# A split first transfer, a rounding moved to VectorE, and another order of the narrow products

## The chip, the cores and the metric

The kernel runs on one core of a Trainium2 chip. Times are microseconds on the device (us). A run's time is that of one execution of the program; the span of a profile runs from its first to its last instruction.

## What is computed

The input x has 128 samples of 32 heads by 512 values. Two residual steps follow each other. The first adds a linear map with a low-rank correction whose factor A is picked by each sample's label. The second adds, for each head, a causal convolution along the 512 values with a kernel K of that head, a skip term, and a mask by each sample's length.

```python
x = x + (einsum('bsi,oi->bso', x, W)
         + 0.5 * einsum('bsr,or->bso', einsum('bsi,bir->bsr', x, lora_A[label]), lora_B_w))
K = 2.0 * einsum('hn,hnl->hl', Ct, exp(P)).real          # one kernel of 512 taps per head
y = irfft(rfft(x, 1024) * rfft(K, 1024))[..., :512] + x * D[:, None]
x = x + y * (arange(512)[None, :] < length[:, None])[:, None, :]
```

## The kernel before

The 512 values of a head lie in four chunks of 128 on the partitions (CH = 4, P = 128), and the 128 samples are the free axis. So every product is a 128x128 weight tile against a moving tile of 128 columns for each (head, chunk) pair. To keep precision, each fp32 operand is split in two fp32r parts, a rounded one (`_hi`) and the rest (`_lo`), and a product is three: hi by hi, lo by hi, hi by lo.

**The start.** W is not used as it comes. TensorE first multiplies A of label 0 by B for each chunk c (the fold, `fold_ps[c]`, four tiles of 32 rows each, read from the one tile `ab_raw`), and VectorE adds half of it to W's chunk (`w_raw`, the scalar_tensor_tensor in `split_chunk`). Chunk 0 of W is added in two halves of 256 columns (`w_parts`), the others in one piece. ScalarE rounds each piece to `w_hi` and x's chunk to `x_hi` (`split_chunk_hi`), VectorE takes the rests `x_lo` and `w_lo`. TensorE's first stage, `chunk(0)` to `chunk(3)`, multiplies these for the first group of four heads. `chunk(0)` waits for `x_hi` of chunk 0 and the first half of `w_hi`, and before its third product for the second half of `w_hi`. The loads of `ab_raw` and then of x's four first chunks stand on SyncE's queue, those of W on ScalarE's.

**Pass 1** goes on over eight groups of four heads with products of 512 columns. Meanwhile K is made on VectorE, ScalarE and GpSimd and stored to `k_pad` in memory.

**Pass 2** (`pass2`) takes the 32 heads one by one. For each the Toeplitz tiles `t_hi` and `t_lo` stand in four blocks by lag, and `xs_hi`, `xs_lo` are the moving parts. The block of lag 0 meets 512 columns, lag 1 384, lag 2 256 and lag 3 128, all summed in one PSUM bank of the pair `y2_ps` (which the profile calls `k_ps`). Lag by lag, three products each: twelve products and twelve weight loads a head. The last head is written out apart, in two halves. VectorE merges a head's sum into x under the mask, and SyncE stores it.

The order on each engine is as the code is written; engines wait for each other by semaphores alone.

Of the kernel before, what the change touches and what calls it, by code (L numbers as in the profile page):

```python
# [13 lines left out]
P = 128  # L14
H = 32
L = 512
CH = L // P
NLAB = 5
RANK = 32
# [10 lines left out]
GH = 4  # L30
GROUPS = H // GH
HALF = L // 2
RAW, TR, XR, LEAD = 4, 5, 4, 3
# [13 lines left out]
def conditioned_residual(nc, xt, idx, wt, a_lab, ab, log_dt, ssm, d_skip, out):  # L47
    ctx = ExitStack()
    with ctx:
# [6 lines left out]
        def sem(name):  # L56
            return ctx.enter_context(nc.semaphore(name))


        x_all = sb("x_all", [P, H, L])  # L60

        x_hi = sb("x_hi", [P, 2 * GH, L], F32R)
        x_lo = sb("x_lo", [P, 2 * GH, L], F32R)

        xs_hi = sb("xs_hi", [P, XR, L], F32R)
        xs_lo = sb("xs_lo", [P, XR, L], F32R)
# [9 lines left out]
        ab_raw = sb("ab_raw", [P, P + L])  # L76
# [49 lines left out]
        t_hi = sb("t_hi", [P, TR, L], F32R)  # L126
# [13 lines left out]
        x_load = [sem(f"x_load{g}") for g in range(1, GROUPS)]  # L140
        w_load = [sem(f"w_load{c}") for c in range(CH)]
        a_load = sem("a_load")
        ab_load = sem("ab_load")
        idx_load = sem("idx_load")
        prm_load = sem("prm_load")
        t_load = [sem(f"t_load{i}") for i in range(RAW)]
# [14 lines left out]
        w_lo_done = sem("w_lo_done")  # L161
        dve_own = sem("dve_own")
        masks = sem("masks")
        x_hi_done = sem("x_hi_done")
        x_lo_done = sem("x_lo_done")
        x_used = sem("x_used")
# [40 lines left out]
        def cols(c):  # L207
            return slice(c * P, (c + 1) * P)
# [5 lines left out]
            return slice(GH * (g % 2), GH * (g % 2) + GH)  # L214


        def split_count(g):
            return CH + 2 * g


        def w_parts(c):
            return ((1, slice(0, HALF)), (2, slice(HALF, L))) if c == 0 else ((c + 2, slice(0, L)),)
# [11 lines left out]
        @block.sync  # L234
        def _(sp):
            def load_x(g):
                sp.dma_start(x_all[:, heads_of(g), :], xt[:, heads_of(g), :]).then_inc(x_load[g - 1], 16)

            sp.dma_start(ab_raw[:], ab).then_inc(ab_load, 16)
            for c in range(CH):  # L240
                sp.dma_start(x_all[:, 0:GH, cols(c)], xt[:, 0:GH, cols(c)]).then_inc(x0_load[c], 16)
            for half in range(2):
                rows = slice(NST * half, NST * half + NST)
                sp.dma_start(logs[rows, 1, :], ssm[:, 0, :]).then_inc(prm_load, 16)
                sp.dma_start(prm[rows, :, :], ssm[:, 1:4, :]).then_inc(prm_load, 16)
            sp.dma_start(logs[:, 0, :], log_dt.rearrange("(o h) -> o h", o=1).broadcast_to([P, H]))\
                .then_inc(prm_load, 16)
            sp.dma_start(d_all[:], d_skip.rearrange("(o h) -> o h", o=1).broadcast_to([P, H])).then_inc(prm_load, 16)
            load_x(1)
            sp.dma_start(idx_i[:], idx.rearrange("(o t) b -> o t b", o=1).broadcast_to([P, 2, P])).then_inc(idx_load, 16)  # L250
            for g in range(2, GROUPS):
                load_x(g)
            sp.wait_ge(consts, 3)
            sp.dma_start(k_pad[:, L:PADK], zeros[:]).then_inc(zeros_stored, 16)

            sp.wait_ge(k_out, 1)
            for j in range(HG):
                rows = k_pad[j:H:HG, 0:L].rearrange("g (a b) -> a g b", b=LB)
                sp.dma_start(rows, k_sb[LA * j:LA * j + LA, :, LB * j:LB * j + LB]).then_inc(k_stored, 16)
            sp.wait_ge(k_stored, 16 * HG)  # L260
            sp.wait_ge(zeros_stored, 16)

            def load_t(k):

                if k >= RAW:
                    sp.wait_ge(t_lo_done, k - RAW + 1)
                window = bass.AP(k_pad.tensor, k * PADK, [[1, P], [1, L]])
                sp.dma_start(t_raw[:, k % RAW, :], window).then_inc(t_load[k % RAW], 16)


            AHEAD = RAW + TR - 2
            for k in range(AHEAD):
                load_t(k)
            for h in range(LAST):
                if AHEAD + h < H:
                    load_t(AHEAD + h)
                sp.wait_ge(o_done, h + 1)
                sp.dma_start(out[:, h, :], x_all[:, h, :]).then_inc(out_stored, 16)
            sp.wait_ge(o_done, H)
            sp.dma_start(out[:, LAST, HALF:L], x_all[:, LAST, HALF:L]).then_inc(out_stored, 16)  # L280
            sp.wait_ge(o_done, H + 1)
            sp.dma_start(out[:, LAST, 0:HALF], x_all[:, LAST, 0:HALF]).then_inc(out_stored, 16)
            sp.wait_ge(out_stored, 16 * (H + 1))
# [127 lines left out]
        def _(act):  # L411
# [3 lines left out]
                act.dma_start(w_raw[:, c, :], wt[cols(c), :]).then_inc(w_load[c], 16)  # L415

            def split_chunk_hi(c):
                act.wait_ge(x0_load[c], 16)
                s.copy(x_hi[:, 0:GH, cols(c)], x_all[:, 0:GH, cols(c)]).then_inc(x_hi_done, 1)
                for n, o in w_parts(c):  # L420
                    act.wait_ge(w_sum, n)
                    s.copy(w_hi[:, c, o], w_raw[:, c, o]).then_inc(w_hi_done, 1)
# [5 lines left out]
                split_chunk_hi(c)  # L428
            act.wait_ge(a_diffed, 1)
            s.copy(a_hi[:], a_diff[:]).then_inc(a_hi_done, 1)  # L430
            act.wait_ge(ab_load, 16)
            s.mul(b_stack[:], ab_raw[0:3 * RANK, P:P + L], LORA_SCALING).then_inc(b_hi_done, 1)

            def split_x_hi(g, pair):
# [86 lines left out]
        def _(pe):  # L521
# [8 lines left out]
            pe.wait_ge(consts, 2)  # L530
            for c in range(CH):
                mm(fold_ps[c][:, cols(c)], ident[:], ident2[:], start=True, stop=False, skip_group_check=True)
            pe.wait_ge(ab_load, 16)
            for c in range(CH):
                r = slice(RANK * c, RANK * c + RANK)
                mm(fold_ps[c], ab_raw[r, 0:P], ab_raw[r, P:P + L], start=False, stop=True,  # L536
                   skip_group_check=True).then_inc(folded, 1)
# [24 lines left out]


            def chunk(c):
                pe.wait_ge(x_hi_done, c + 1)
                for d in range(CH):
                    if c > 0 or d % 2 == 0:
                        pe.wait_ge(w_hi_done, c + 2 if c > 0 else d // 2 + 1)
                    mm(by_head(y_ps[:, d, :]), w_hi[:, c, cols(d)], moving(x_hi, 0, c), start=(c == 0), stop=False,  # L569
                       skip_group_check=True)  # L570
                pe.wait_ge(x_lo_done, c + 1)
                for d in range(CH):
                    mm(by_head(y_ps[:, d, :]), w_hi[:, c, cols(d)], moving(x_lo, 0, c), start=False, stop=False,  # L573
                       skip_group_check=True)
                pe.wait_ge(w_lo_done, c + 1)
                for d in range(CH):
                    last = mm(by_head(y_ps[:, d, :]), w_lo[:, c, cols(d)], moving(x_hi, 0, c), start=False, stop=False,  # L577
                              skip_group_check=True)
                return last

            def low_group(g):
                pe.wait_ge(x_hi_done, split_count(g))
                pe.wait_ge(x_lo_done, split_count(g))
                if g >= 2:
                    pe.wait_ge(low_read, (NLAB - 1) * (g - 1))
                for c in range(CH):
                    last = low(g, c)
                last.then_inc(low_done, 1)
# [42 lines left out]

            def pass2(h):
                wait_head(h)
                for lag in range(CH):
                    last = blocks(y2_ps[h % 2][:, lag * P:L], h, lag, lag, CH - lag, lag == CH - 1)
                last.then_inc(y2_done, 1)

            chunk(0)
# [1 line left out]
            chunk(2)  # L640
            pe.wait_ge(a_hi_done, 1)
            pe.wait_ge(a_lo_done, 1)
            pe.wait_ge(x_hi_done, CH)
            pe.wait_ge(x_lo_done, CH)
            pe.wait_ge(w_sum, CH + 1)
            for c in range(CH):
# [49 lines left out]
        def _(dve):  # L696
# [8 lines left out]
            def split_chunk(c):  # L705

                dve.wait_ge(folded, c + 1)
                dve.wait_ge(w_load[c], 16)
                for _, o in w_parts(c):
                    v.scalar_tensor_tensor(w_raw[:, c, o], fold_ps[c][:, o], LORA_SCALING, w_raw[:, c, o],  # L710
                                           ALU.mult, ALU.add).then_inc(w_sum, 1)
                dve.wait_ge(x_hi_done, c + 1)
                v.tensor_tensor(x_lo[:, 0:GH, cols(c)], x_all[:, 0:GH, cols(c)],
                                f32(x_hi[:, 0:GH, cols(c)]), ALU.subtract).then_inc(x_lo_done, 1)
                dve.wait_ge(w_hi_done, c + 2)
                v.tensor_tensor(w_lo[:, c, :], w_raw[:, c, :], f32(w_hi[:, c, :]), ALU.subtract)\
                    .then_inc(w_lo_done, 1)
# [23 lines left out]
            step(v.tensor_scalar(lab_mask[:], lab_f, lab_of[:], None, ALU.is_equal))  # L741

            def split_x_lo(g, pair):
                dve.wait_ge(x_hi_done, split_count(g - 1) + pair + 1)
                b, h = GH * (g % 2) + 2 * pair, GH * g + 2 * pair
                v.tensor_tensor(x_lo[:, b:b + 2, :], x_all[:, h:h + 2, :], f32(x_hi[:, b:b + 2, :]),  # L746
                                ALU.subtract).then_inc(x_lo_done, 1)
# [157 lines left out]
```

## Time and profile before

| | us |
|---|---|
| median of 3 runs | 192.66 (192.64 to 196.02) |
| the profiled execution | 192.58 |
| its span, first to last instruction | 190.9 |

The profiled execution is 1.7 us longer than its span and 0.08 us below the median. A row of a timeline gives the start, the length, the engine, the line and the operation, and in brackets the idle time ahead of it and what ended that. PE is TensorE's products and PEld its weight loads, which run beside products.

### The profile page before, as it was taken

How to read it: one execution, taken by the hardware profiler on the slowest of the kernel's cores; microseconds unless marked ns; L12 is line 12 of the kernel's file. 1: busy time of each engine (PE TensorE's matmuls, PEld its weight loads, DVE VectorE, ACT ScalarE, POOL GpSimd, SP SyncE). 2: the span in 40 equal slices, each digit the busy share in tenths (PEclk: the TensorE clock that was granted, in tenths of full speed). 3: DMA queues.
4: the chain of work that ended last, by engine and by line, in shares of the span. 5: the costliest groups of instructions: out<-in, count | busy, mean ns of one | idle time of the engine just before them, and what ended most of it. 6: DMA issues, size and time to landing. Idle time of an engine off the chain costs nothing.

```text
span 190.9 us, 2653 instructions
## 1 busy us (share of the span) xinstructions
PE 185.6 (97%) x933; PEld 156.6 (82%) x933; DVE 125.9 (66%) x164; ACT 91.3 (48%) x144; POOL 68.7 (36%) x111
## 2 busy tenths in 40 slices
PE   7799999999999999999999999999999999999994
PEld 2487887888888888888888888888999999999993
DVE  0599979458977048858607407279987777786743
ACT  2456066254148754154463312766565656565600
POOL 6038840000000268100000000379886666676600
PEclk9999999999999999999999999999999999999999
DMA  6999990000000000000001600045988788897433
GB/s 191 349 366 422 424 408 11 0 0 2 3 2 0 0 2 3 0 0 0 0 3 34 200 0 0 0 146 167 309 285 295 282 261 291 277 274 270 181 139 138
DMA packets 14797, 27.35 MB, mean 143 GB/s; under 512 B 2592, under 2 KB 5056, under 8 KB 13888
## 3 DMA queue, kind: packets, MB, share of 16 engines
q1 hardware_dynamic: 14064, 25.81, 39.1%
q10 hardware_dynamic: 720, 1.38, 2.1%
q8 instruction: 7, 0.11, 0.3%
q14 instruction: 6, 0.05, 0.1%
HBM read 18.71 MB, written 8.47 MB: 142 GB/s over the span
## 4 chain that ended last, share of the span: by engine, by line
PE 95%; DVE 2%; ACT 1%; issue 0%
PE y_ps L553 13%; PE y_ps L554 12%; PE y_ps L555 12%; PE k_ps L620 10%; PE k_ps L621 10%; PE k_ps L622 10%; PE low_ps L547 4%; PE low_ps L549 4%; PE low_ps L548 4%; PE y_ps L560 4%; PE y_ps L569 2%; PE y_ps L573 2%; PE y_ps L577 2%; PE low_ps L526 2%; PE k_ps L536 1%; PE k_ps L555 1%
## 5 line engine op out<-in xcount | busy, mean ns | idle before, releaser
L406 POOL TENSOR_TENSOR t_lo<-w_raw,t_hi 128x512 fp32r<-128x512 f32 x32 | 44.3, 1393 | 38.0 <-ACT t_hi L468 37.8
L620 PE MATMUL k_ps<-xs_hi,t_hi 128*128 128x128 f32 (+3 forms) x130 | 41.5, 319 | 0.2 <-DVE x_all L829 0.2
L621 PE MATMUL k_ps<-xs_hi,t_lo 128*128 128x128 f32 (+3 forms) x130 | 41.5, 319 | 0.0
L622 PE MATMUL k_ps<-xs_lo,t_hi 128*128 128x128 f32 (+3 forms) x130 | 41.4, 318 | 0.0
L553 PE MATMUL y_ps<-x_hi,w_hi 128*128 128x512 f32 x104 | 40.6, 391 | 0.0
L555 PE MATMUL y_ps<-x_lo,w_hi 128*128 128x512 f32 x104 | 40.6, 391 | 0.0
L554 PE MATMUL y_ps<-x_hi,w_lo 128*128 128x512 f32 x104 | 40.6, 390 | 0.0
L757 DVE COPY_PREDICATED low_sel<-lab_mask,low_ps 32x512 f32<-32x512 int32 x32 | 23.3, 729 | 25.0 <-PE low_ps L549 24.1
L829 DVE COPY_PREDICATED x_all<-len_mask,k_ps 128x512 f32<-128x512 int32 x31 | 23.3, 750 | 13.1 <-PE k_ps L622 13.0
L769 DVE TENSOR_TENSOR xs_lo<-x_all,xs_hi 128x512 fp32r<-128x512 f32 x32 | 28.1, 883 | 4.6 <-ACT xs_hi L462 4.6
L462 ACT CAST xs_hi<-x_all 128x512 fp32r<-128x512 f32 x32 | 19.9, 622 | 19.7 <-PE k_ps L622 19.7
L454 ACT COPY x_all<-y_ps 128x512 f32<-128x512 f32 x30 | 16.6, 591 | 24.3 <-PE y_ps L560 24.3
L620 PEld LDWEIGHTS k_ps<-xs_hi,t_hi 128*128 128x128 f32 x130 | 24.5, 189 | 1.7 <-issue 0.3
L622 PEld LDWEIGHTS k_ps<-xs_lo,t_hi 128*128 128x128 f32 x130 | 24.6, 189 | 1.4
L621 PEld LDWEIGHTS k_ps<-xs_hi,t_lo 128*128 128x128 f32 x130 | 24.6, 189 | 1.2
L553 PEld LDWEIGHTS y_ps<-x_hi,w_hi 128*128 128x128 f32 x104 | 19.5, 188 | 4.6 <-ACT x_all L454 0.4
L554 PEld LDWEIGHTS y_ps<-x_hi,w_lo 128*128 128x128 f32 x104 | 19.5, 188 | 4.3
L555 PEld LDWEIGHTS y_ps<-x_lo,w_hi 128*128 128x128 f32 x104 | 19.5, 188 | 4.1
L468 ACT CAST t_hi<-w_raw 128x512 fp32r<-128x512 f32 x32 | 19.8, 620 | 0.8 <-DMA w_raw<-k_pad 0.8
L448 ACT CAST low_stack<-low_sel 32x512 fp32r<-32x512 f32 x8 | 5.0, 620 | 28.1 <-DVE low_sel L757 28.1
L746 DVE TENSOR_TENSOR x_lo<-x_all,x_hi 128x1024 fp32r<-128x1024 f32 x14 | 16.9, 1240 | 0.3
L324 POOL TENSOR_TENSOR tmp<-ex 128x32 f32<-128x32 f32 x1 | 0.2, 240 | 38.4 <-ACT phase L500 38.4
(132 smaller groups left out, 221.4 us busy)
## 6 DMA issues: line engine op xcount, KB each, us to landing
w_raw<-k_pad SPq DMA_DIRECT2D x32, 256.0 KB, 4.2
out<-x_all SPq DMA_DIRECT2D x31, 256.0 KB, 3.3
x_all<-in_xt SPq DMA_DIRECT2D x7, 1024.0 KB, 12.3
w_raw<-in_wt ACTq DMA_DIRECT2D x4, 256.0 KB, 5.4
x_all<-in_xt SPq DMA_DIRECT2D x4, 256.0 KB, 7.2
ab_raw<-in_ab SPq DMA_DIRECT2D x1, 320.0 KB, 3.7
a_raw<-in_a_lab ACTq DMA_DIRECT2D x1, 320.0 KB, 7.4
out<-x_all SPq DMA_DIRECT2D x2, 128.0 KB, 1.8
```

The costliest lines, as they stand in the source:

```text
L406: g.tensor_tensor(t_lo[:, k % TR, :], t_raw[:, k % RAW, ::-1], f32(t_hi[:, k % TR, :]), ALU.subtract).then_inc(t_lo_done, 1)
L462: s.copy(xs_hi[:, h % XR, :], x_all[:, h, :]).then_inc(xs_hi_done, 1)
L468: s.copy(t_hi[:, k % TR, :], t_raw[:, k % RAW, ::-1]).then_inc(t_hi_done, 1)
L553: mm(o, w_hi[:, c, cols(d)], moving(x_hi, g, c), start=(c == 0), stop=False, skip_group_check=True)
L554: mm(o, w_lo[:, c, cols(d)], moving(x_hi, g, c), start=False, stop=False, skip_group_check=True)
L555: return mm(o, w_hi[:, c, cols(d)], moving(x_lo, g, c), start=False, stop=False, skip_group_check=True)
L620: mm(o, t_hi[:, u, cols(lag)], xs_hi[:, b, x], start=(lag == 0), stop=False, skip_group_check=True)
L621: mm(o, t_lo[:, u, cols(lag)], xs_hi[:, b, x], start=False, stop=False, skip_group_check=True)
L622: return mm(o, t_hi[:, u, cols(lag)], xs_lo[:, b, x], start=False, stop=ends, skip_group_check=True)
L757: v.copy_predicated(low_sel[:], lab_mask[rows, :].unsqueeze(1).to_broadcast([RANK, GH, P]), low_ps[rows, g % 2, :].rearrange("p (h b) -> p ...
L769: v.tensor_tensor(xs_lo[:, h % XR, :], x_all[:, h, :], f32(xs_hi[:, h % XR, :]), ALU.subtract).then_inc(xs_lo_done, 1)
L829: v.copy_predicated(x_all[:, h, :], mask, y2_ps[h % 2]).then_inc(o_done, 1)
```

## The change

Three edits. The load of `ab_raw` becomes two transfers on SyncE's queue, of rows 0 to 31 and of rows 32 to 127, with a semaphore each; the fold of chunk 0 waits for the first alone, that of chunk 1 for the second. The rounding of x's chunk 0 goes from ScalarE to VectorE, where it stands between the two halves of W's chunk 0; `x_hi_done` then counts one less, which the counts elsewhere follow. In pass 2 each of the three products of lag 3 stands right behind the product of lag 0 that has the same two parts.

```diff
-            sp.dma_start(ab_raw[:], ab).then_inc(ab_load, 16)
+            sp.dma_start(ab_raw[0:RANK, :], ab[0:RANK, :]).then_inc(ab_load[0], 16)
+            sp.dma_start(ab_raw[RANK:P, :], ab[RANK:P, :]).then_inc(ab_load[1], 16)
...
             def split_chunk_hi(c):
-                act.wait_ge(x0_load[c], 16)
-                s.copy(x_hi[:, 0:GH, cols(c)], x_all[:, 0:GH, cols(c)]).then_inc(x_hi_done, 1)
+                if c > 0:
+                    act.wait_ge(x0_load[c], 16)
+                    s.copy(x_hi[:, 0:GH, cols(c)], x_all[:, 0:GH, cols(c)]).then_inc(x_hi_done, 1)
...
-            pe.wait_ge(ab_load, 16)
             for c in range(CH):
+                if c < 2:
+                    pe.wait_ge(ab_load[c], 16)
...
             def chunk(c):
-                pe.wait_ge(x_hi_done, c + 1)
+                if c == 0:
+                    pe.wait_ge(x0_hi_done, 1)
+                else:
+                    pe.wait_ge(x_hi_done, c)
...
             def pass2(h):
                 wait_head(h)
-                for lag in range(CH):
-                    last = blocks(y2_ps[h % 2][:, lag * P:L], h, lag, lag, CH - lag, lag == CH - 1)
+                o, b, u = y2_ps[h % 2], h % XR, h % TR
+                near, far = cols(0), cols(CH - 1)
+                for t, x in ((t_hi, xs_hi), (t_lo, xs_hi), (t_hi, xs_lo)):
+                    mm(o, t[:, u, near], x[:, b, :], start=(t is t_hi and x is xs_hi), stop=False, skip_group_check=True)
+                    mm(o[:, far], t[:, u, far], x[:, b, near], start=False, stop=False, skip_group_check=True)
+                for lag in (1, 2):
+                    last = blocks(o[:, lag * P:L], h, lag, lag, CH - lag, lag == 2)
                 last.then_inc(y2_done, 1)
...
-                for _, o in w_parts(c):
+                for n, o in w_parts(c):
                     v.scalar_tensor_tensor(w_raw[:, c, o], fold_ps[c][:, o], LORA_SCALING, w_raw[:, c, o],
                                            ALU.mult, ALU.add).then_inc(w_sum, 1)
-                dve.wait_ge(x_hi_done, c + 1)
+                    if n == 1:
+                        dve.wait_ge(x0_load[0], 16)
+                        v.tensor_copy(x_hi[:, 0:GH, cols(0)], x_all[:, 0:GH, cols(0)]).then_inc(x0_hi_done, 1)
+                if c == 0:
+                    dve.wait_ge(x0_hi_done, 1)
+                else:
+                    dve.wait_ge(x_hi_done, c)
```

On VectorE, at the program's start, before the change (`warm` is a tile of zeros, the shapes are partitions by elements):

```order
L719 MEMSET warm 128x256
L710 SCALAR_TENSOR_TENSOR w_raw<-k_ps,w_raw 128x256 x2
L713 TENSOR_TENSOR x_lo<-x_all,x_hi 128x4x128
L716 TENSOR_TENSOR w_lo<-w_raw,w_hi 128x512
L710 SCALAR_TENSOR_TENSOR w_raw<-k_ps,w_raw 128x512
```

The same place in the changed kernel:

```order
L743 MEMSET warm 128x256
L728 SCALAR_TENSOR_TENSOR w_raw<-k_ps,w_raw 128x256
L732 CAST x_hi<-x_all 128x4x128
L728 SCALAR_TENSOR_TENSOR w_raw<-k_ps,w_raw 128x256
L737 TENSOR_TENSOR x_lo<-x_all,x_hi 128x4x128
L740 TENSOR_TENSOR w_lo<-w_raw,w_hi 128x512
```

A copy that rounds x now stands between the two halves of W's chunk 0; the second half, x_lo and w_lo stand behind it.

On TensorE, at the first head of pass 2 and the beginning of the second, before the change (the third word of a row is the product's result, the last its moving columns; each has a weight load of its own):

```order
L620 MATMUL k_ps<-xs_hi,t_hi 128x256
L621 MATMUL k_ps<-xs_hi,t_lo 128x256
L622 MATMUL k_ps<-xs_lo,t_hi 128x256
L620 MATMUL k_ps<-xs_hi,t_hi 128x128
L621 MATMUL k_ps<-xs_hi,t_lo 128x128
L622 MATMUL k_ps<-xs_lo,t_hi 128x128
L620 MATMUL k_ps<-xs_hi,t_hi 128x512
```

One head there in the changed kernel, and the first product of the next:

```order
L650 MATMUL k_ps<-xs_hi,t_hi 128x512
L651 MATMUL k_ps<-xs_hi,t_hi 128x128
L650 MATMUL k_ps<-xs_hi,t_lo 128x512
L651 MATMUL k_ps<-xs_hi,t_lo 128x128
L650 MATMUL k_ps<-xs_lo,t_hi 128x512
L651 MATMUL k_ps<-xs_lo,t_hi 128x128
L632 MATMUL k_ps<-xs_hi,t_hi 128x384
L633 MATMUL k_ps<-xs_hi,t_lo 128x384
L634 MATMUL k_ps<-xs_lo,t_hi 128x384
L632 MATMUL k_ps<-xs_hi,t_hi 128x256
L633 MATMUL k_ps<-xs_hi,t_lo 128x256
L634 MATMUL k_ps<-xs_lo,t_hi 128x256
```

The narrow products, three in a row before with the next head's wide one behind them, now stand one by one between wide ones; the head ends with its products of 256 columns.

## Rows read from the trace of the kernel before

**Rows 1.** The page: busy time of each engine over the span

```profile
PE 185.6 (97%) x933; PEld 156.6 (82%) x933; DVE 125.9 (66%) x164; ACT 91.3 (48%) x144; POOL 68.7 (36%) x111
```

**Rows 2.** Busy time by stretch: PE, PEld, DVE, ACT, POOL, clock, DMA, GB/s

```profile
150.00:188.00 38.00, 38.00 (x246) 35.54 (x244) 26.59 (x38) 18.95 (x33) 21.21 (x17) 1.00 0.71 240
```

**Rows 3.** The chain that ended last, one piece at the start

```profile
7.33 0.41 ACT w_hi L422
```

**Rows 4.** Timeline of the start: start, length, engine, line, operation

```profile
6.26 0.62 ACT L419 CAST x_hi<-x_all 128x512 fp32r<-128x512 f32 x1 [1.31 <-DMA x_all<-in_xt]
6.87 0.76 DVE L710 SCALAR_TENSOR_TENSOR w_raw<-k_ps,w_raw 128x256 f32<-128x256 f32 x2 [5.69 <-PE low_ps L536]
...
7.33 0.74 ACT L422 CAST w_hi<-w_raw 128x256 fp32r<-128x256 f32 x2 [0.45 <-DVE w_raw L710]
7.54 0.68 DVE L713 TENSOR_TENSOR x_lo<-x_all,x_hi 128x512 fp32r<-128x512 f32 x1
...
7.85 0.76 PEld L569 LDWEIGHTS y_ps<-x_hi,w_hi 128*128 128x128 f32 x4 [2.57 <-ACT x_hi L419]
7.88 1.17 PE L569 MATMUL y_ps<-x_hi,w_hi 128*128 128x512 f32 x4 [1.03 <-ACT w_hi L422]
...
8.14 0.69 DVE L716 TENSOR_TENSOR w_lo<-w_raw,w_hi 128x512 fp32r<-128x512 f32 x1
...
8.65 0.88 PEld L573 LDWEIGHTS y_ps<-x_lo,w_hi 128*128 128x128 f32 x4
```

**Rows 5.** Timeline just ahead of the fold, on TensorE

```profile
4.52 0.31 PE L532 MATMUL low_ps<-ident 128*128 128x128 bf16 x1
...
4.76 0.28 PEld L536 LDWEIGHTS k_ps<-ab_raw 32*128 32x128 f32 x1 [0.20 <-issue]
```

**Rows 6.** SyncE's queue: the issue of the first load

```profile
0.79 0.39 SPq L239 DMA_DIRECT2D ab_raw<-in_ab  x1
```

**Rows 7.** DMA issues: count, KB each, median us from issue to landing

```profile
ab_raw<-in_ab SPq DMA_DIRECT2D x1, 320.0 KB, 3.7
```

**Rows 8.** VectorE's groups by line and shape: total busy us, mean ns

```profile
L713 DVE TENSOR_TENSOR x_lo<-x_all,x_hi 128x512 fp32r<-128x512 f32 x4 | 2.7, 681 | 0.0
...
L774 DVE TENSOR_SCALAR phase<-phase,shift 128x512 f32<-128x512 f32 x1 | 0.5, 486 | 0.0
...
L737 DVE CAST idx_f<-idx_i 128x256 f32<-128x256 int32 x1 | 0.3, 308 | 0.0
```

**Rows 9.** Timeline of pass 2, TensorE's products around the end of a head

```profile
149.73 0.45 PE L620 MATMUL k_ps<-xs_hi,t_hi 128*128 128x512 f32 x1
...
151.35 0.22 PE L620 MATMUL k_ps<-xs_hi,t_hi 128*128 128x128 f32 x1
151.41 0.28 PE L621 MATMUL k_ps<-xs_hi,t_lo 128*128 128x128 f32 x1
151.52 0.28 PE L622 MATMUL k_ps<-xs_lo,t_hi 128*128 128x128 f32 x1
151.63 0.45 PE L620 MATMUL k_ps<-xs_hi,t_hi 128*128 128x512 f32 x1
```

**Rows 10.** Timeline of pass 2, TensorE's weight loads in the same place

```profile
151.23 0.19 PEld L620 LDWEIGHTS k_ps<-xs_hi,t_hi 128*128 128x128 f32 x1
151.35 0.19 PEld L621 LDWEIGHTS k_ps<-xs_hi,t_lo 128*128 128x128 f32 x1
151.46 0.19 PEld L622 LDWEIGHTS k_ps<-xs_lo,t_hi 128*128 128x128 f32 x1
151.57 0.19 PEld L620 LDWEIGHTS k_ps<-xs_hi,t_hi 128*128 128x128 f32 x1
151.68 0.19 PEld L621 LDWEIGHTS k_ps<-xs_hi,t_lo 128*128 128x128 f32 x1
151.92 0.19 PEld L622 LDWEIGHTS k_ps<-xs_lo,t_hi 128*128 128x128 f32 x1
152.15 0.19 PEld L620 LDWEIGHTS k_ps<-xs_hi,t_hi 128*128 128x128 f32 x1
```

More of the change, by code:

```diff
@@ L142, in conditioned_residual @@
         a_load = sem("a_load")
-        ab_load = sem("ab_load")
+        ab_load = [sem(f"ab_load{i}") for i in range(2)]
         idx_load = sem("idx_load")
@@ L163, in conditioned_residual @@
         masks = sem("masks")
+        x0_hi_done = sem("x0_hi_done")
         x_hi_done = sem("x_hi_done")
@@ L214, in buf_of, with hi_count, lo_count @@
             return slice(GH * (g % 2), GH * (g % 2) + GH)
-        def split_count(g):
+        def hi_count(g):
+            return CH - 1 + 2 * g
+        def lo_count(g):
             return CH + 2 * g
@@ L430, in _ @@
             s.copy(a_hi[:], a_diff[:]).then_inc(a_hi_done, 1)
-            act.wait_ge(ab_load, 16)
+            act.wait_ge(ab_load[0], 16)
+            act.wait_ge(ab_load[1], 16)
             s.mul(b_stack[:], ab_raw[0:3 * RANK, P:P + L], LORA_SCALING).then_inc(b_hi_done, 1)
@@ L581, in low_group @@
             def low_group(g):
-                pe.wait_ge(x_hi_done, split_count(g))
-                pe.wait_ge(x_lo_done, split_count(g))
+                pe.wait_ge(x_hi_done, hi_count(g))
+                pe.wait_ge(x_lo_done, lo_count(g))
                 if g >= 2:
@@ L642, in _ @@
             pe.wait_ge(a_lo_done, 1)
-            pe.wait_ge(x_hi_done, CH)
+            pe.wait_ge(x_hi_done, CH - 1)
             pe.wait_ge(x_lo_done, CH)
@@ L743, in split_x_lo @@
             def split_x_lo(g, pair):
-                dve.wait_ge(x_hi_done, split_count(g - 1) + pair + 1)
+                dve.wait_ge(x_hi_done, hi_count(g - 1) + pair + 1)
                 b, h = GH * (g % 2) + 2 * pair, GH * g + 2 * pair
```

## The prediction

> **What bounds the kernel now.** I read the page first, then busy time by stretch, then the chain at the start, then timelines of the two places that the change touches. The page says that TensorE is busy for 185.6 of 190.9 us [rows 1]. In the stretch of pass 2 it is busy for all of 38.00 us at a granted clock of 1.00 [rows 2]. So neither another engine nor a wait sets the time there, and only the spacing of TensorE's own instructions can change it. The one stretch in which TensorE waits is the start: the chain goes from VectorE's sum of W's first half (6.87) over ScalarE's rounding of it (7.33, 0.41 long) to the first product at 7.88 [rows 3, 4]. From there it has work to the end, so a start that is later by some time ends later by that time.
>
> **How pass 2 is spaced.** The ends of products in a profile are modelled, so I go by starts, and by the loads. A head takes 151.63 - 149.73 = 1.90 us [rows 9]. The loads tell what a product really costs. Those at 151.35, 151.46, 151.57 and 151.68 are 0.11 us apart, though the narrow product that starts at 151.35 is followed in the record by the next one after 0.06 [rows 9, 10]. So a narrow product passes in 0.06 and then stands 0.05 until the next one's weights are in. The third of these gaps belongs to the first wide product of the next head: its load goes out at 151.57, and the load behind it, at 151.68, marks its start.
>
> The second thing to see is when a load goes out. After the load of 151.68 the loader is free at about 151.79 (0.11 later), but the next load waits until 151.92, when the next wide product starts, and the one after that until 152.15 [rows 10]. So one set of weights is fetched ahead and no more: the load for a product starts when the product before it starts. Then the time from one product to the next is the longer of two things, the passing of its own columns (0.23 for 512) and the load of the weights that come next (0.11).
>
> **The change, part by part. The order in pass 2: nothing.** By that rule a head costs the sum over its products of the longer of both, and as all loads take the same time, the sum doesn't depend on the order. Before, three narrow products hide too little of the load behind them: that of the second narrow, of the third, and of the next wide one. After, a narrow product's own weights do come in under a wide one, but the load behind each narrow one (the second wide, the third wide, the first of 384 columns) is hidden by 0.06 of narrow columns, just as before. Three gaps of 0.05 before and three after. The trace of before shows both new neighbours: a wide product behind a narrow one at 151.57 to 151.68 (0.11), and a narrow one with its weights already in, whose load went out at 151.23 under the last product of 256 columns [rows 10]. The number of products, loads and columns stays. The y2_done signal comes from a product of 256 columns now and not from a narrow one; the sum is complete at the same time, and VectorE's merge behind it has no say in a stretch where TensorE never waits.
>
> What is left unknown is a hundredth per product: the first wide product behind a narrow one took 0.24 (151.68 to 151.92), the next 0.23. Two more of the former a head are 0.02, over 31 heads (the last is not changed) 0.6 us; I take nothing, and 0.6 to either side for the range.
>
> **The first load in two: nothing.** Issued at 0.79, it landed 3.7 us later, at 4.49 [rows 6, 7]. TensorE still had the last of its small identity products to start then, at 4.52 [rows 5], so that an earlier landing finds it busy. The fold's first load goes out at 4.76, with 0.20 of idle time put down to issue and not to a transfer. If those 0.24 us (4.52 to 4.76) were the transfer's after all, the first sum of W would come up to 0.24 earlier; I count 0, and keep 0.24 for the low end. The second transfer moves each load behind it on SyncE's queue by one issue, 0.39 [rows 6]. x's chunk 0, on which ScalarE started at 6.26 [rows 4], then lands by 6.65, still ahead of VectorE's use of it at 7.21 (next paragraph). The later chunks of x come as much later; ScalarE's rounding of chunk 1, which follows below, has room for it. The wait for the second part stands ahead of the folds of chunks 1 to 3, and VectorE reads chunk 1's only after 8.74 (0.60 behind its w_lo at 8.14, as x_lo takes 0.60 from its start to the next one's [rows 4]), so it hides.
>
> **The rounding on VectorE: 0.30 later.** ScalarE rounded x at 6.26 and had it by 6.88; then it waited for VectorE's sum for 0.45 us [rows 4]. So this rounding was off the path, and what moves it onto VectorE puts it on the path. VectorE starts the two halves of W at 6.87 and half of 0.67 later, at 7.21 (the next instruction starts at 7.54). The new copy of 512 elements goes between. No fp32r copy by VectorE is in the trace. The nearest row is an operation with one fp32 source of the same 512 elements, 486 ns; below it stands a cast of 256 elements with 308 ns, above it the 681 ns of an operation with two sources [rows 8]. I take 0.49, as only that row has both the one source and the size. The Trainium skill (VectorE: DVE Perf Modes, "What auto-detection actually checks") says that an operation with one source, source and result in SBUF and even or equal outer sizes, can run at double rate, which two sources can't; the rows 486 and 681 agree, and without the double rate the copy would cost as the longer row.
>
> With 0.49 the copy ends at 7.70, before ScalarE ends the first half of w_hi (7.33 + 0.41 = 7.74), so the first product keeps its 7.88. But the second half of W starts later by the copy less its overlap with the next instruction (x_lo: 0.68 long, next start after 0.60, so 0.08): 7.21 + 0.41 = 7.62. ScalarE starts 0.46 behind VectorE's start (6.87 to 7.33): 8.08, and ends at 8.49. TensorE's load came 0.11 behind the end of the rounding it waited for (7.74 to 7.85), so the third product's load goes out at 8.60. Before it went out at 8.65 less two products of 0.23, at 8.19, and as a load goes out when the product ahead starts, the third product started one product later, at 8.42. Now it starts one load (0.11) after 8.60, at 8.71. That is 0.29, say 0.30 later, with nothing behind it to win it back. At 0.31 for the copy the same steps give 0.11, at 0.68 they give 0.48.
>
> Is something else late next? x_lo starts half of 0.67 behind the second sum, at 7.95, and w_lo 0.60 later, at 8.55; TensorE asks for x_lo two products after the third and for w_lo six after it, so both hide. ScalarE's rounding of x's chunk 1 begins at about 8.65 by the later landing and lasts 0.62, to 9.27. The sum of W's chunk 1 starts 0.60 behind w_lo, at 9.15, and takes about as long as x_lo, 0.68; its rounding starts by 9.87 and is done at 10.49. TensorE has ten products of chunk 0 from 8.71 on, 2.3 us, so chunk 1's first product is due at 11.0 and its load 0.23 earlier, at 10.8. Chunk 1 isn't late, with 0.2 to spare after the 0.11 from a rounding to a load.
>
> **The sum.** 192.58 (the profiled execution) + 0 + 0 + 0.30 = 192.88. The median stands 0.08 above that execution; I give 192.9.
>
> **The rivals.** *The narrow loads are hidden after all.* If more than one load could run ahead of the products, the three gaps of a head would close: 3 x 0.05 x 31 = 4.7 us, and the time would be 188.2. The loader that sits idle from 151.79 to 151.92 speaks against it. The Trainium skill (TensorE: Matmul & The Clock Gate, "Step-by-step: what each phase is for") says that a 64-deep window pulls weight loads ahead of running products when they go to the background buffer; read as several loads ahead, that is this rival, and read as one buffer, my forecast. The rows show the second. Chance 0.09.
>
> *A load that stands alone costs more.* In a run of narrow products each load follows another at once; after a wide one the loader starts from rest. If then its whole recorded 0.19 counted and not 0.11, each narrow product would cost 0.08 more: 3 x 0.08 x 31 = 7.4 us, 200.3. It decides from the first narrow product of the first head. Against it: the load of 151.35 also came after a load that was done (151.23 + 0.11 = 151.34), and the next followed at 151.46. Chance 0.03.
>
> *The first part of the load does bring the fold forward.* Then the start comes 0.24 earlier, and with the copy's 0.30 or its lower 0.11 the time is 192.6 or 192.4. The label "issue" and the landing at 4.49 ahead of 4.52 speak against it; it is inside the range and changes no verdict. Chance 0.12.
>
> **How the numbers follow.** The forecast has the remaining 0.76. The range: down from 192.9 by 0.43 (an early fold and a short copy, -0.13 instead of 0.30) and 0.6 of pass 2, to 191.9; up by 0.18 (a long copy) and 0.6, to 193.7. It holds the forecast and the early fold, 0.88, less what both may miss of their edges; the two rivals of pass 2 lie outside. Faster by over 2% (under 188.8) is the first rival, 0.09; slower by over 2% the second, 0.03; the rest, 0.88, is within 2%, which is about what a measurement of this kernel can tell from no change.
>
> **What would show it.** In the profile of the changed kernel: the period of a head in pass 2 still 1.90; loads behind narrow products 0.11 apart and behind wide ones 0.23; the fold's first load at 4.76; VectorE's copy about 0.49 long; TensorE's first product near 7.88, and its third standing about 0.3 for the second half of w_hi; the end of pass 2 later by as much. A head of 1.75 would prove the order wrong here, a head above 1.95 the second rival; a fold that starts well before 4.76, or a first product before 7.6, would prove the start wrong.

## The result, and the profile after

The changed kernel takes 194.76 us, the median of 18 runs (193.17 to 196.94). The kernel before takes 192.66 in 18 runs beside them (191.92 to 196.02). The ratio is 1.0079, with a 95% interval of 1.0049 to 1.0109; it leaves out the executions that lie over 1.5% above the fastest of their kernel. The forecast was 192.9, with a range of 191.9 to 193.7. "Within 2%" came true, but the time lies above the range: the change costs 1.5 us by the ratio and 2.1 by the medians, where the forecast had 0.3.

The 18 executions differ more than those of before, and they sort by the mean granted clock of TensorE. With 0.998 to 1.00 they take 193.17 to 194.15, apart from one of 196.48 (the last section shows that a mean of 1.00 can hide a low level at the start; whether it does there isn't known). With 0.991 they take 193.94 to 196.01, and with 0.982 or 0.983 195.58 to 196.94. Seven of the 18 are of the first kind, five of the second and six of the third. The profiled execution is one of the third kind: it took 196.94 for a span of 195.2 us. So its rows show the loss at its full size, 4.36 us above the profiled execution of before (192.58), and the median of all has about half of that.

The page of the changed kernel, busy times and clock in 40 slices:

```profile
PE 187.5 (96%) x933; PEld 158.4 (81%) x933; DVE 126.2 (65%) x165; ACT 90.5 (46%) x143; POOL 69.4 (36%) x111
...
PEclk9859999999999999999999999999999999999999
```

Against [rows 1] the count of instructions differs by one on two engines only (VectorE has one more, ScalarE one less), while the span is 4.3 us longer. The clock's second and third slice, about 5 to 15 us, say where to look. The chain that ended last in the changed kernel, its pieces at the start (start, length, what):

```profile
1.70 7.99 DMA x_all<-in_xt
...
10.20 2.08 PE y_ps L581 x4
12.27 1.71 PE y_ps L585 x4
13.98 1.51 PE y_ps L589 x4
15.49 0.91 PE y_ps L581 x4
```

Before, the chain came to the first product over VectorE's sum and ScalarE's rounding of W [rows 3]; now it comes over a load, x's chunk 0, issued at 1.70. Four products of chunk 0 take 1.5 to 2.1 us, four of chunk 1 0.91. The timeline of the same start in the changed kernel:

```profile
1.24 0.41 SPq L244 DMA_DIRECT2D ab_raw<-in_ab  x1
...
1.70 3.04 SPq L246 DMA_DIRECT2D x_all<-in_xt  x4
...
4.76 0.33 PEld L545 LDWEIGHTS k_ps<-ab_raw 32*128 32x128 f32 x2 [0.20 <-issue]
...
4.78 3.23 SPq L249 DMA_DIRECT2D logs<-in_ssm  x1
...
5.96 0.42 DVE L728 SCALAR_TENSOR_TENSOR w_raw<-k_ps,w_raw 128x256 f32<-128x256 f32 x1 [4.78 <-PE k_ps L545]
...
9.71 0.43 DVE L732 CAST x_hi<-x_all 128x512 fp32r<-128x512 f32 x1 [3.33 <-DMA x_all<-in_xt]
...
10.20 2.08 PE L581 MATMUL y_ps<-x_hi,w_hi 128*128 128x512 f32 x4 [3.66 <-DVE x_hi L732]
...
10.97 0.58 PEld L581 LDWEIGHTS y_ps<-x_hi,w_hi 128*128 128x128 f32 x2 [0.27 <-ACT w_hi L429]
...
15.33 1.08 PE L581 MATMUL y_ps<-x_hi,w_hi 128*128 128x512 f32 x4
```

W's first sum is ready earlier than before (5.96 against 6.87 [rows 4]), but VectorE then stands 3.33 us for x's chunk 0 and TensorE 3.66 for the copy of it. The first product starts at 10.20 instead of 7.88 [rows 4]: 2.32 us. Chunk 1 starts at 15.33; in the same view of before it starts at 10.72:

```profile
10.72 1.07 PE L569 MATMUL y_ps<-x_hi,w_hi 128*128 128x512 f32 x4
```

So chunk 0's twelve products take 5.13 instead of 2.84, another 2.29; within it the third product's load also waits 0.27 for the second half of w_hi. Together this is 4.61 us at chunk 1, slightly more than the whole loss. The windows view of the changed kernel (busy time of PE, PEld, DVE, ACT and POOL, clock, DMA share, GB/s) tells the rest of why the products are slow:

```profile
8.30:15.10 6.80, 4.90 (x12) 3.80 (x13) 5.29 (x10) 2.98 (x6) 0.74 (x2) 0.50 0.78 202
15.20:20.00 4.80, 4.80 (x23) 3.96 (x22) 4.62 (x9) 3.35 (x6) 4.21 (x8) 1.00 0.87 360
150.00:188.00 38.00, 38.00 (x241) 35.47 (x241) 27.82 (x40) 21.24 (x38) 24.42 (x19) 1.00 0.75 258
```

TensorE is granted 0.50 of its clock from 8.30 to 15.10, that is 1.2 GHz instead of 2.4. Before, it had 1.00 in those 6.80 us. The engine stands for 3.66 us ahead of the first product, and the clock falls within that wait. In pass 2 TensorE is still busy for all of 38.00 us at 1.00, as in [rows 2]. Pass 2's loads in the changed kernel (L651 is the narrow product):

```profile
154.33 0.19 PEld L651 LDWEIGHTS k_ps<-xs_hi,t_hi 128*128 128x128 f32 x1
154.56 0.19 PEld L650 LDWEIGHTS k_ps<-xs_hi,t_lo 128*128 128x128 f32 x1
154.67 0.19 PEld L651 LDWEIGHTS k_ps<-xs_hi,t_lo 128*128 128x128 f32 x1
154.90 0.19 PEld L650 LDWEIGHTS k_ps<-xs_lo,t_hi 128*128 128x128 f32 x1
...
156.23 0.19 PEld L651 LDWEIGHTS k_ps<-xs_hi,t_hi 128*128 128x128 f32 x1
```

From one head's first narrow load to the next head's is 156.23 - 154.33 = 1.90 us, the period of [rows 9]. Loads are 0.23 apart while a wide product passes and 0.11 while a narrow one does: against [rows 10] the gaps have moved and none has closed. Pass 2 begins at 131.10 and ends with the span 64.1 later; before it was 126.57 and 64.3. The loss is all at the start.

Last, the DMA issues of the changed kernel (count, KB each, median us from issue to landing):

```profile
w_raw<-in_wt ACTq DMA_DIRECT2D x4, 256.0 KB, 5.8
x_all<-in_xt SPq DMA_DIRECT2D x4, 256.0 KB, 9.5
...
ab_raw<-in_ab SPq DMA_DIRECT2D x1, 80.0 KB, 2.5
```

The first part of A0 and B (`ab_raw` holds A of label 0 and B) now lands 2.5 us after its issue at 0.79, at 3.3, instead of 4.49 [rows 7], and the fold's first load still goes out at 4.76 [rows 5]. x's four loads take 9.5 in the median; before it was 7.2, and W's took 5.4.

### The profile page after: what moved, and what is told of

Its sections match the earlier page's. It is cut to its first block, busy times and chain, and to the rows that moved or that the text cites. A ratio compares the mean times of both kernels' runs of the same rounds, so it can differ in the third digit from the quotient of the medians.

```text
span 195.2 us, 2655 instructions
## 1 busy us (share of the span) xinstructions
PE 187.5 (96%) x933; PEld 158.4 (81%) x933; DVE 126.2 (65%) x165; ACT 90.5 (46%) x143; POOL 69.4 (36%) x111
## 4 chain that ended last, share of the span: by engine, by line
PE 91%; DMA 4%; DVE 2%; ACT 1%; SPq 0%; issue 0%
PE y_ps L562 12%; PE y_ps L563 12%; PE y_ps L564 12%; PE k_ps L650 12%; PE k_ps L632 5%; PE k_ps L633 5%; PE k_ps L634 5%; DMA x_all<-in_xt 4%; PE low_ps L556 4%; PE low_ps L557 4%; PE low_ps L558 4%; PE y_ps L569 4%; PE k_ps L651 3%; PE y_ps L581 2%; PE y_ps L585 2%; PE y_ps L589 2%
## 5 line engine op out<-in xcount | busy, mean ns | idle before, releaser
L632 PE MATMUL k_ps<-xs_hi,t_hi 128*128 128x384 f32 (+1 forms) x68 | 22.3, 327 | 0.0
L633 PE MATMUL k_ps<-xs_hi,t_lo 128*128 128x384 f32 (+1 forms) x68 | 20.8, 306 | 0.0
L634 PE MATMUL k_ps<-xs_lo,t_hi 128*128 128x384 f32 (+1 forms) x68 | 20.8, 305 | 0.0
L448 ACT CAST x_hi<-x_all 128x1024 fp32r<-128x1024 f32 x14 | 14.0, 1054 | 0.0
L632 PEld LDWEIGHTS k_ps<-xs_hi,t_hi 128*128 128x128 f32 x68 | 12.8, 188 | 1.3
L650 PE MATMUL k_ps<-xs_hi,t_lo 128*128 128x512 f32 x31 | 13.8, 445 | 0.0
```

The lines of the kernel that those rows point to most:

```text
L632: mm(o, t_hi[:, u, cols(lag)], xs_hi[:, b, x], start=(lag == 0), stop=False, skip_group_check=True)
L633: mm(o, t_lo[:, u, cols(lag)], xs_hi[:, b, x], start=False, stop=False, skip_group_check=True)
L634: return mm(o, t_hi[:, u, cols(lag)], xs_lo[:, b, x], start=False, stop=ends, skip_group_check=True)
L650: mm(o, t[:, u, near], x[:, b, :], start=(t is t_hi and x is xs_hi), stop=False, skip_group_check=True)
```

## The experiments

The expectations name the theories by letters. A puts the loss down to the first load's split, B to VectorE's rounding, C to the order in pass 2. Of A there are two kinds: by A1 it is one transfer more ahead of x's chunk 0, whatever its size, and by A2 the uneven cut in rows. By T the loads on ScalarE's queue take turns with SyncE's on the same DMA engines and go ahead; by U SyncE's queue itself is slow. Each ratio is against runs of the kernel before on the same chip.

**Parts of the change alone.** e1 puts the split alone into the kernel before:

```diff
-sp.dma_start(ab_raw[:], ab).then_inc(ab_load, 16)
+sp.dma_start(ab_raw[0:RANK, :], ab[0:RANK, :]).then_inc(ab_load[0], 16)
+sp.dma_start(ab_raw[RANK:P, :], ab[RANK:P, :]).then_inc(ab_load[1], 16)
 for c in range(CH):
+    if c < 2: pe.wait_ge(ab_load[c], 16)
```

> Only the first load is split; rounding and pass 2 as before. Theory A (the split pushes the load of x's chunk 0 back, TensorE waits for it, and in some executions its clock falls): nearly all of the loss is here, 193.5 to 195, with the first product later than 7.9 us and executions in which the granted clock is below 1. Theory B (VectorE, which waits in order for x's chunk 0 between the halves of W, makes the loss): the split alone costs nothing, 192.3 to 192.8. Theory C (the new order in pass 2 costs): 192.6.

Measured: 195.63, ratio 1.0127 (1.0059 to 1.0195). The timeline of e1:

```profile
9.97 0.62 ACT L420 CAST x_hi<-x_all 128x512 fp32r<-128x512 f32 x1 [5.41 <-DMA x_all<-in_xt]
...
11.04 1.19 PE L572 MATMUL y_ps<-x_hi,w_hi 128*128 128x512 f32 x2 [4.21 <-ACT w_hi L423]
```

The late chunk of x is there without the other two parts, and the clock with it (0.982 to 0.991 in its four executions). The split alone makes the whole loss, and 0.6 more than the 195 that A gave at most.

e2 has the rounding on VectorE alone, that is after's code with the first load in one piece again and with pass 2 as before:

```diff
-sp.dma_start(ab_raw[0:RANK, :], ab[0:RANK, :]).then_inc(ab_load[0], 16)
-sp.dma_start(ab_raw[RANK:P, :], ab[RANK:P, :]).then_inc(ab_load[1], 16)
+sp.dma_start(ab_raw[:], ab).then_inc(ab_load, 16)
```

> Only VectorE's rounding of x's chunk 0; one first load and pass 2 as before. Theory A: x's chunk lands at about 6.2 and the loss is the 0.3 of the prediction, 192.9. Theory B: 193.2 to 195. Theory C: 192.9.

Measured: 192.34, ratio 0.9988 (0.996 to 1.0015). e3 has only the new order of pass 2:

```diff
-for lag in range(CH):
-    last = blocks(y2_ps[h % 2][:, lag * P:L], h, lag, lag, CH - lag, lag == CH - 1)
+for t, x in ((t_hi, xs_hi), (t_lo, xs_hi), (t_hi, xs_lo)):
+    mm(o, t[:, u, near], x[:, b, :], ...)
+    mm(o[:, far], t[:, u, far], x[:, b, near], ...)
+for lag in (1, 2):
+    last = blocks(o[:, lag * P:L], h, lag, lag, CH - lag, lag == 2)
```

> Only the new order in pass 2. Theories A and B: a head still takes 1.90 us and the time is that of before, 192.6 within 0.3. Theory C: 194.

Measured: 192.55, ratio 1.0008 (0.9981 to 1.0035). e4 has both, so it is after with only the split taken back (the edit of e2's diff).

> The whole change with the split taken back. Theory A: the loss falls to 0.3, 192.9. Theory B: the loss stays, 194. Theory C: 194.

Measured: 192.57, ratio 0.9995 (0.9966 to 1.0023). With e1 to e4, B and C fall: neither part nor both together make a difference that can be measured. The timeline of e4, where the fold is as slow as in the profile of before and the first sum of W only 0.10 earlier (6.77 against 6.87 [rows 4]), shows what is left of the rounding's price:

```profile
6.77 0.42 DVE L725 SCALAR_TENSOR_TENSOR w_raw<-k_ps,w_raw 128x256 f32<-128x256 f32 x1 [5.59 <-PE low_ps L542]
7.11 0.42 DVE L729 CAST x_hi<-x_all 128x512 fp32r<-128x512 f32 x1
...
7.45 0.42 DVE L725 SCALAR_TENSOR_TENSOR w_raw<-k_ps,w_raw 128x256 f32<-128x256 f32 x1
...
7.78 1.32 PE L578 MATMUL y_ps<-x_hi,w_hi 128*128 128x512 f32 x4 [1.04 <-ACT w_hi L428]
...
7.90 0.41 ACT L428 CAST w_hi<-w_raw 128x256 fp32r<-128x256 f32 x1 [0.26 <-DVE w_raw L725]
...
8.36 0.30 PEld L578 LDWEIGHTS y_ps<-x_hi,w_hi 128*128 128x128 f32 x2 [0.31 <-ACT w_hi L428]
...
10.79 1.07 PE L578 MATMUL y_ps<-x_hi,w_hi 128*128 128x512 f32 x4
```

The third product's load waits 0.31 for the second half of w_hi, about as forecast. The first product starts 0.10 earlier than before (7.78), by the 0.10 of the sum. From it to chunk 1, at 10.79, it is 3.01 us where before it was 2.84: 0.17 is what the rounding costs between these two profiles.

**What of the split costs.** e5 cuts the load of the kernel before into equal halves; chunks 0 and 1 of the fold wait for the first, 2 and 3 for the second:

```diff
-sp.dma_start(ab_raw[:], ab).then_inc(ab_load, 16)
+sp.dma_start(ab_raw[0:P // 2, :], ab[0:P // 2, :]).then_inc(ab_load[0], 16)
+sp.dma_start(ab_raw[P // 2:P, :], ab[P // 2:P, :]).then_inc(ab_load[1], 16)
+    if c % 2 == 0: pe.wait_ge(ab_load[c // 2], 16)
```

> The kernel before with the first load cut into two equal halves of 64 rows (chunks 0 and 1 of the fold wait for the first, 2 and 3 for the second). Theory A1 (any transfer more ahead of x's chunk 0 on SyncE's queue pushes it back): as with 32 and 96 rows, 194 to 196, x's chunk 0 in use only after 9 us. Theory A2 (the uneven cut leaves one part of the DMA with more to do): 192.4, x's chunk 0 by 6.7.

Measured: 197.15, ratio 1.0249 (1.0204 to 1.0294). e6 cuts nothing; in the kernel before it moves the 16 KB load of d_all (D of the skip term) from behind x's chunks to ahead of them:

```diff
 sp.dma_start(ab_raw[:], ab).then_inc(ab_load, 16)
+sp.dma_start(d_all[:], d_skip....broadcast_to([P, H])).then_inc(prm_load, 16)
 for c in range(CH): sp.dma_start(x_all[:, 0:GH, cols(c)], ...)
```

> The kernel before with the first load whole, but the small load of d_all moved from behind x's chunks to ahead of them, so that x is issued one transfer later and nothing is cut. Theory A1: 194 to 196. Theory A2: 192.4 to 192.8.

Measured: 197.33, ratio 1.0255 (1.021 to 1.03). The timeline of e6:

```profile
1.22 0.42 SPq L240 DMA_DIRECT2D d_all<-in_d_skip  x1
...
3.93 3.75 SPq L245 DMA_DIRECT2D logs<-in_ssm  x1
...
9.23 0.62 ACT L419 CAST x_hi<-x_all 128x512 fp32r<-128x512 f32 x1 [4.59 <-DMA x_all<-in_xt]
...
10.30 2.05 PE L569 MATMUL y_ps<-x_hi,w_hi 128*128 128x512 f32 x4 [4.49 <-ACT w_hi L422]
```

An unrelated 16 KB in that place, with A0 and B in one piece, costs as much as the split: A2 falls. A1 holds as to the place, while the times of e5 and e6 lie above the 196 that it gave. x's chunk 0 is used at 9.23 instead of 6.26, although it is issued only 0.46 later. That e6 loses in the same way as after isn't shown, though. The windows view has from 4.00 to 5.50 (the last two numbers are the DMA share and GB/s), first in e6, then in before:

```profile
4.00:5.50 1.50, 1.50 (x13) 0.67 (x11) 0.00 (x0) 0.64 (x1) 0.33 (x4) 1.00 0.15 47
...
4.00:5.50 1.50, 1.50 (x9) 0.88 (x11) 0.00 (x0) 0.95 (x1) 0.34 (x4) 1.00 1.10 370
```

In e6 the DMA engines are nearly idle there, with loads of both queues under way. 66 of the 71 packets that SyncE's queue begins in that time have 128 B, as the rows of d_all have: while the small load's pieces pass, both queues stand nearly still, and no run shows why. In after the share in that stretch is 1.06.

e7 leaves after as it is but issues x's chunk 0 between the two parts:

```diff
 sp.dma_start(ab_raw[0:RANK, :], ab[0:RANK, :]).then_inc(ab_load[0], 16)
-sp.dma_start(ab_raw[RANK:P, :], ab[RANK:P, :]).then_inc(ab_load[1], 16)
 for c in range(CH):
     sp.dma_start(x_all[:, 0:GH, cols(c)], ...)
+    if c == 0:
+        sp.dma_start(ab_raw[RANK:P, :], ab[RANK:P, :]).then_inc(ab_load[1], 16)
```

> The changed kernel with x's chunk 0 issued between the two parts of the first load. Theory A1: x's chunk 0 is issued when it was before, lands by about 6.2, and the loss is gone, 192.0 to 192.6; the fold of chunks 1 to 3 comes up to 0.7 later and hides. Theory A2: the loss stays with x's chunk 1, 193 to 196.

Measured: 195.24, ratio 1.0153 (1.0122 to 1.0184). The timeline of e7:

```profile
6.40 0.43 DVE L733 CAST x_hi<-x_all 128x512 fp32r<-128x512 f32 x1
...
7.98 0.18 PEld L546 LDWEIGHTS k_ps<-ab_raw 32*128 32x128 f32 x1 [2.85 <-DMA ab_raw<-in_ab]
```

Now x's chunk 0 is in time (6.40), but the second part of A0 and B, issued at 1.70 in its place, is as late as x was. The fold of chunks 1 to 3 stands ahead of chunk 0's products in TensorE's order, so TensorE waits there instead, 2.85 us. A1 had this hide and the loss gone, and its time is missed. Whatever SyncE issued third, at 1.70, came late, in after, e6 and e7 alike.

e8 keeps TensorE busy in the wait of after, by 16 products of zeros behind the fold into a tile that chunk 0's first product overwrites:

```diff
+for _ in range(16):
+    mm(y_ps[:, 0, :], warm[:, 0:P], warm[:], start=True, stop=True)
 chunk(0)
```

> The changed kernel with 16 more warm products of 512 columns on TensorE between the fold and its first stage (their result is overwritten), 3.5 to 6.8 us in which it would else wait for x. If the falling clock makes most of the loss: the granted clock stays at 1.00 after the fold, and the time falls below that of the changed kernel by 1 to 3 us in its worse executions, to 193.5 to 195. If the wait alone makes it: no gain, 194.5 to 196.5.

Measured: 194.63 (194.55 to 195.40 in four executions), ratio 1.0126 (1.009 to 1.0161). Its windows view, and VectorE's copy in its timeline:

```profile
6.50:15.10 8.60, 8.60 (x42) 5.66 (x39) 6.35 (x12) 3.61 (x7) 0.00 (x0) 1.00 0.86 262
...
8.54 0.43 DVE L735 CAST x_hi<-x_all 128x512 fp32r<-128x512 f32 x1 [1.38 <-DMA x_all<-in_xt]
```

The clock stays at 1.00 in the stretch, and its mean is 1.00 in all four executions (a mean that can miss a low level at the start), where after has 0.982 to 0.991 in 11 of 18. Chunk 1 starts at 13.18 by the chain instead of 15.49. None of the four lies at 196 or above, where seven of after's 18 are; four are few, and as many drawn from after's would all lie below about one time in seven. The median is that of after all the same: the late transfer is a loss without the clock, and how much of the 1.26% the 16 products themselves cost can't be told from the run, since they hold TensorE until 10.42 while x's chunk 0 is used at 8.54.

**Why x comes late.** e9 takes after and issues x's chunk 0 on ScalarE's queue, right behind W's chunk 0; e10 does the same to the kernel before:

```diff
-for c in range(CH):      # SyncE
+for c in range(1, CH):
+    if c == 0:           # ScalarE, behind its load of W's chunk 0
+        act.dma_start(x_all[:, 0:GH, cols(0)], xt[:, 0:GH, cols(0)]).then_inc(x0_load[0], 16)
```

> The changed kernel, with x's chunk 0 issued on ScalarE's queue, right behind W's chunk 0, instead of on SyncE's. Theory T (the DMA serves the two queues in turns, so a transfer that starts one place later on SyncE's queue waits for several of W's) and its rival U (SyncE's queue itself is slow once a transfer more stands ahead, whatever ScalarE's does) both let x's chunk 0 land by about 6. T: x's chunk 1 has one place less ahead of it and comes by 8.5, so the loss is gone, 192 to 192.8. U: x's chunk 1 stays late, at 9 to 11, 193.5 to 195.

> The kernel before with x's chunk 0 on ScalarE's queue behind W's chunk 0, one first load. T: x's chunk 0 by 5.5, chunk 1 by 7.5, W's chunks 1 to 3 up to 0.7 later; 191.3 to 192.4. U: x's chunk 1 as before at 8.2, 192.4.

Measured: e9 192.85, ratio 1.0007 (0.9984 to 1.003), with a clock of 0.998 to 1.00 in all ten executions; e10 192.31, ratio 0.9988 (0.9966 to 1.0009). The timeline of e9:

```profile
6.88 1.31 PE L583 MATMUL y_ps<-x_hi,w_hi 128*128 128x512 f32 x4 [1.03 <-ACT w_hi L429]
```

With the split still in and x's chunk 0 on the other queue, the first product starts at 6.88 and the loss is gone. x's chunk 1 lands at 8.64, where T had 8.5 and U 9 to 11. In e10 it lands at 5.50, now second on SyncE's queue (T had 7.5, U 8.2), and the two times given for e10 are too close to tell T from U.

e11 takes after and leaves x where it is, but takes rivals away from it: W's chunks 2 and 3 and a_raw move from ScalarE's queue to SyncE's, behind x's chunks 1, 2 and 3. e12 does the same to the kernel before:

```diff
 for c in range(CH):      # SyncE
     sp.dma_start(x_all[:, 0:GH, cols(c)], ...)
+    if c in (1, 2):
+        sp.dma_start(w_raw[:, c + 1, :], wt[cols(c + 1), :]).then_inc(w_load[c + 1], 16)
+sp.dma_start(a_raw[:], a_lab).then_inc(a_load, 16)
-for c in range(CH):      # ScalarE's loads of W; a_raw behind them is gone too
+for c in range(2):
```

> The changed kernel with W's chunks 2 and 3 and the load of A taken off ScalarE's queue and issued on SyncE's, behind x's chunks 1, 2 and 3: the same transfers, but x's chunk 0 shares the DMA only with W's chunks 0 and 1. T: x's chunk 0 lands by 6.2 and chunk 1 by 7.5 in spite of the split, and the time falls to 191.5 to 192.6. U: x's chunk 0 stays at 7 to 9.7, and the time at 194 or more.

> The kernel before with the same three loads moved to SyncE's queue. T: x's chunk 0 by 5.7, chunk 1 by 7, 191.3 to 192.3. U: no gain, 192.4 to 193.

Measured: e11 192.73, ratio 1.0022 (0.9985 to 1.0059); e12 192.19, ratio 0.9975 (0.9952 to 0.9997). From e11, the timeline:

```profile
6.63 0.41 DVE L734 CAST x_hi<-x_all 128x512 fp32r<-128x512 f32 x1
...
7.29 1.31 PE L583 MATMUL y_ps<-x_hi,w_hi 128*128 128x512 f32 x4 [0.82 <-ACT w_hi L432]
```

And its DMA issues:

```profile
x_all<-in_xt SPq DMA_DIRECT2D x4, 256.0 KB, 5.2
w_raw<-in_wt ACTq DMA_DIRECT2D x2, 256.0 KB, 3.6
```

x's chunk 0 is issued at 1.70 on SyncE's queue behind both parts, exactly as in after, and is in time; its loads take 5.2 in the median instead of 9.5. So SyncE's queue isn't slow by itself, and U falls. What made x late in after was the loads that ScalarE's queue had under way beside it, as T has it, though the times of e9 and e11 lie 0.05 and 0.13 above T's ranges. The Trainium skill (DMA: Bandwidth & Descriptors, "Queues, rings and completion order") says that each DMA engine serves the queues that have work for it in turns. The DMA view of after from 4.50 to 8.50 agrees so far that packets of both queues begin in it (by their bytes q1 is SyncE's queue and q10 ScalarE's):

```profile
q10 hardware_dynamic: 427, 0.82, 58.1%
q1 hardware_dynamic: 1022, 0.51, 45.0%
```

In e11 ScalarE's queue has 25 packets there and SyncE's 1828. But the sharing isn't the whole delay. A load counts its semaphore up in sixteen parts, and the trace keeps when each part landed. Of x's chunk 0 fifteen parts are in by 6.99 in after, and the last at 9.69; in e1 by 7.34 and at 9.95, in before by 6.11 and at 6.24, in e11 all by 6.29. So most of the delay in after and e1 is one part that comes 2.6 to 2.7 us behind the others. In e5 and e6 all sixteen are spread out, from 7.20 to 9.37 and from 6.92 to 9.21.

One thing holds in all profiles but two: the third load of SyncE's queue, whatever it is, lands at 7.93 to 9.95, and in before too (8.22, x's chunk 1). Only in e11 (6.29) and e12 (6.79) is it earlier. The split, and d_all's load in e6, moved x's chunk 0 from second place to third.

e11 isn't quite clear of the loss: four of its ten executions have a clock of 0.991 and take 194.26 to 195.32, the other six 191.85 to 192.74. Of 35 runs of before beside them one has 0.991.

e12 lies 0.25% below before. The interval just leaves out 1, which one among twelve can do by chance, so a gain isn't shown.

## Why the prediction was wrong

**Pass 2: right.** No change forecast, 0.6 to either side; the period is 1.90 as before, the loads stand 0.23 and 0.11 apart with three short ones a head, and e3 gives 1.0008. The rule from the rows, one set of weights fetched ahead, held for the new order, and the two rivals of pass 2 (188.2 and 200.3) fall.

**The fold: right.** Its first load stayed at 4.76 though its part landed at 3.3. In the profile of after the first sum of W is 0.9 earlier, at 5.96, but this isn't the split's doing: it is 5.83 in e6, which has none. The fold's passes take 0.5 us in some executions and 1.0 in others.

**The rounding: right in kind, too large.** The third product's load waited 0.31 in e4 for the second half of w_hi, but from the first product to chunk 1 the rounding costs 0.17 and not 0.30. Two terms were too large. The copy took 0.42 where 0.49 was forecast, and the second sum began 0.34 behind it (7.11 to 7.45) where 0.41 was forecast. The load then went out 0.05 behind the end of the rounding it waited for (8.31 to 8.36), and not 0.11. The time agrees: e2's upper bound, 1.0015, is 0.29 us, and e4's, 1.0023, 0.44.

**The second transfer: this is the step that failed.** I wrote that it "moves each load behind it on SyncE's queue by one issue, 0.39", and that x's chunk 0 "then lands by 6.65". The issue did move by about as much (0.47), but the chunk was used at 9.71: 3.45 us later than at 6.26 and not 0.39. In e8's profile, whose clock is at 1.00, it was used at 8.54, 2.28 later. I took a landing to move with its issue, as if the queue had the DMA engines to itself. Beside it ScalarE's queue was loading W (four times 256 KB) and a_raw (320 KB), and in the first 8.30 us of before the DMA engines are busy for 0.83 of the time. e1 shows that the second transfer alone does it, and e11 that it takes W's later loads and a_raw on the other queue. Before had rows for the price, since its third load on SyncE's queue is x's chunk 1:

```profile
1.23 2.37 SPq L241 DMA_DIRECT2D x_all<-in_xt  x4
...
8.25 0.62 ACT L419 CAST x_hi<-x_all 128x512 fp32r<-128x512 f32 x1 [0.18 <-DMA x_all<-in_xt]
```

The second of these four issues stands at 1.70, where x's chunk 0 stands in after, and ScalarE waited for that load until 8.25. So x's chunk 0 in that place was due at about 8.2, not at 6.65. I used the 8.25, but for chunk 1 alone. The median of 7.2 us for x's loads, against 3.7 for A0 and B [rows 7], was a further sign that they were waiting.

That the time stayed within 2% is luck, then, as the reason given for it failed: e5, which cuts the same load at another row, is at 2.5%.

**What followed, and wasn't among the rivals.** I named no case in which x's chunk is late. Had I, the price was still half: the wait of 3.66 us on TensorE is followed by twelve products at 1.2 GHz, which with the third product's wait of 0.27 take 2.29 us more, in the executions where the clock falls. e8, with the engine kept busy, speaks for the fall of the clock following from the wait (four of four executions have a mean of 1.00, where seven of after's 18 have 0.998 or more); that its removal alone would shorten the median isn't shown.

The three parts of the change also meet. In e1 ScalarE's rounding of W stands behind its rounding of x, so that both come after the late chunk, and its first product is at 11.04; in after ScalarE rounds W's first half while VectorE waits, and it is at 10.20. In exchange, VectorE's copy holds the second half of W back. Whether after is faster than e1 for that isn't settled, as their intervals overlap.

**What stays open.** One is why one part of sixteen of x's chunk 0 lands 2.70 us behind the rest in after, and why the third place on SyncE's queue is so much later than the second; the sharing with ScalarE's loads takes part in it, but no run shows how. Another is which of the three loads moved in e11 weighs most. A third is what still lowers the clock in four of e11's executions, whose profiled one is at 0.999.

## What to carry to other kernels

When a transfer is added ahead of others on one queue, don't price it by its issue: ask what the other queues have under way on the same DMA engines at that moment, and which load on the path loses its place to them. The row to look up is that of the load that has the new place before the change. Here the cut of a load cost 0.8% (after) to 2.5% (e5), and 16 KB in rows of 128 B ahead of the first chunk of x cost 2.55%. A wait of TensorE near the start should be priced at its length and, separately, at its length plus the products that follow at half clock.

## What the runs showed of the hardware

Two queues share the DMA engines, and a load issued 0.46 to 0.47 us later on one of them came into use 2.3 to 3.5 us later (x's chunk 0 at 6.26 before, 8.54 in e8, 9.23 in e6, 9.71 in after). Its sixteen parts need not land together: in after the last comes 2.70 us behind the fifteenth. SyncE's own issuing was held up with it: its issue of the small logs load takes 3.23 us in after and 3.75 in e6, against 0.89 before.

After TensorE had stood for 3.66 us its products came 0.43 us apart for five microseconds, at a granted clock of 0.50, before it had 1.00 again.

The record of the granted clock can miss a low level at the very start. In the profiled execution of e5 its mean over the span is given as 1.00, yet its chain at the start reads so:

```profile
10.46 2.04 PE y_ps L572 x4
...
14.21 1.71 PE y_ps L580 x4
15.92 1.25 PE y_ps L572 x4
17.17 0.93 PE y_ps L576 x4
```

Four products in 1.71 us are the 0.43 apart of the 1.2 GHz level, and four in 0.93 that of the other. So the spacing of equal products tells the level more surely than the mean.
